# A gated recurrence on one core: VectorE takes x's sums with the bias from PSUM, update gates ahead of tanh, m by chunk and batch, a later wait for y, the last rows not moved

## What is computed

```python
def step(h, x_t):
    fused = sigmoid(concat([x_t, h]) @ w_W + w_b)
    hidden_state, output_state = split(fused, 2)
    memory_state = x_t @ wx_W + wx_b + hidden_state * (h @ wh_W + wh_b)
    h_new = output_state * h + (1.0 - output_state) * tanh(memory_state)
    return h_new, h_new
out = x + swapaxes(scan(step, cond_1024, swapaxes(x, 0, 1)), 0, 1)
```

## Time and profile before

| what | value |
|---|---|
| median of three runs | 1776.34 us |
| the profiled execution's own time | 1774.11 us |
| its span, first to last instruction | 1772.1 us |
| mean granted TensorE clock | 0.993 |
| busy share of the span: PE / PEld / DVE / ACT / POOL | 96 / 77 / 66 / 51 / 39 % |

### The profile page before, as it was taken

One profiled execution on the slowest core, in us unless ns is written; L12 is line 12 of the kernel. 1 busy time (PEld: TensorE's weight loads), 2 busy tenths in 40 slices (PEclk: granted clock), 3 DMA queues, 4 the chain that ended last, 5 costly groups with the idle time before them and its releaser, 6 DMA issues.

```text
span 1772.1 us, 211898 instructions
## 1 busy us (share of the span) xinstructions
PE 1697.1 (96%) x94336; PEld 1359.4 (77%) x94336; DVE 1174.3 (66%) x5144; ACT 910.5 (51%) x4749; POOL 694.7 (39%) x2699
## 2 busy tenths in 40 slices
PE   4999999999999999999999999999999999999997
PEld 2777777777777777777777777777777777777775
DVE  3666666666666666666666666666666666666665
ACT  2455555555555555555555555555555555555554
POOL 1334344333443433443343443334434434434433
PEclk8999999999999999999999999999999999999999
DMA  6111111111111111111111111111111111111111
GB/s 188 31 44 48 46 39 38 48 47 44 48 35 45 43 49 46 44 36 47 44 48 46 39 38 48 47 44 48 35 44 43 50 46 44 36 47 44 48 46 38
DMA packets 195513, 83.66 MB, mean 47 GB/s; under 512 B 123568, under 2 KB 194992, under 8 KB 195504
## 3 DMA queue, kind: packets, MB, share of 16 engines
q1 hardware_dynamic: 194448, 82.87, 17.3%
q10 hardware_dynamic: 1056, 0.67, 0.1%
HBM read 49.50 MB, written 33.95 MB: 47 GB/s over the span
## 4 chain that ended last, share of the span: by engine, by line
PE 59%; DVE 25%; issue 5%; POOL 4%; ACT 4%; DMA 1%; POOLq 1%; ACTq 0%; SPq 0%; DVEq 0%
PE ps L265 37%; PE ps L274 12%; PE ps L256 9%; DVE h L464 6%; DVE m_pre L450 5%; DVE turned_rm L439 5%; DVE turned_r L432 4%; DVE m_pre_parts L456 2%; DVE turned_m L435 2%; POOL y L552 2%; ACT m_by L362 2%; ACT h_by L369 2%; POOL h L542 2%; DVE turned_z L443 1%; POOL h L544 1%
## 5 line engine op out<-in xcount | busy, mean ns | idle before, releaser
L265 PE MATMUL ps<-wh,h 128*8 128x64 f32 x65536 | 1209.5, 220 | 56.9 <-DVE h L464 37.1
L265 PEld LDWEIGHTS ps<-wh,h 128*8 128x8 f32 x65536 | 960.3, 93 | 387.6 <-DVE h L464 327.0
L542 POOL TENSOR_TENSOR h<-h 128x16 f32<-128x16 f32 x1026 | 224.9, 219 | 985.1 <-DVE h L464 980.4
L274 PE MATMUL ps<-w_parts,h 128*24 128x128 bf16 x24576 | 531.8, 219 | 0.0
L274 PEld LDWEIGHTS ps<-w_parts,h 128*24 128x24 bf16 x24576 | 431.0, 121 | 0.0
L256 PE MATMUL ps<-wx,x_grp 128*32 128x384 f32 x4096 | 424.4, 486 | 0.0
L464 DVE TENSOR_TENSOR_SCAN h<-h_by,h 128x48 f32<-128x48 f32 x1024 | 258.8, 253 | 216.8 <-ACT h_by L369 216.8
L362 ACT ACTIVATE m_by<-turned_r 128x16 f32<-128x16 f32 x512 | 120.6, 236 | 504.7 <-DVE turned_r L432 504.7
L432 DVE STREAM_TRANSPOSE turned_r<-ps 128x64 f32<-128x64 f32 x512 | 127.9, 250 | 320.4 <-PE ps L265 212.6
L544 POOL TENSOR_TENSOR h<-h 128x16 f32<-128x16 f32 x1026 | 225.1, 219 | 80.4
L443 DVE STREAM_TRANSPOSE turned_z<-ps 128x64 f32<-128x64 f32 x1024 | 237.2, 232 | 2.6 <-PE ps L265 2.5
(11 more groups left out here) (32 smaller groups left out, 531.8 us busy)
## 6 DMA issues: line engine op xcount, KB each, us to landing
x_rows<-xs_biased SPq DMA_DIRECT2D x129, 192.0 KB, 1.9
ahead<-x_rows SPq DMA_DIRECT2D x516, 32.0 KB
ahead<-x_rows SPq DMA_DIRECT2D x1032, 8.0 KB
x_sb<-in_x SPq DMA_DIRECT2D x34, 256.0 KB, 3.1
x_grp<-in_x SPq DMA_DIRECT2D x516, 16.0 KB, 1.7
out_h<-y SPq DMA_DIRECT2D x32, 256.0 KB, 2.7
wx<-in_w_x SPq DMA_DIRECT2D x4, 768.0 KB, 9.7
wh<-in_w_h SPq DMA_DIRECT2D x4, 512.0 KB, 7.3
```

The source lines that it names most:

```text
L265: mm = pe.matmul(ps[Q * j:Q * j + B, bank, 0:W], h_of(s - 1, k), wh[:, k, j, at:at + W], start=False, stop=(k == KC - 1), skip_group_check ...
L274: mm = pe.matmul(ps[Q * j:Q * j + PARTS * B, RM_BANK, 0:2 * W], parts_of(s - 1, k), w_parts[:, k, part, j], start=False, stop=(k == KC - 1 ...
L542: pool.tensor_tensor(mid(1, s, o), mid(0, s, o), mid_top(0, s, o), ALU.subtract).then_inc(left_once[o], 1)
```

## The change

Five edits, in the program's own terms.

1. **x's sums with the bias**: VectorE reads the products from PSUM, adds the bias and writes `xs_biased` in one instruction, behind mix_h(1) of each group's fourth step, after waits for the product and for the rows of the slot that was filled last. ScalarE's take_x, GpSimd's add_bias, the tile xs and the semaphore x_taken are gone; TensorE waits for x_biased in place of x_taken.
2. **Update gates ahead of tanh** on ScalarE, in both halves; mix_h waits for tanh first and then for the gates.
3. **m by chunk and batch**: turned_m and turned_rm, and what is computed from them up to tanh's input, lie by chunk and then batch; before it was batch and then chunk. h stays as it was, so tanh writes in another order of addresses than it reads.
4. **A later wait for y**: VectorE waits at every second step, for y of three steps before; before it was every fourth step, for y of the step before.
5. **SyncE's queue**: the rows of a block's last group are moved at the start of the next block's turn, behind the store of y and the load of x; the transfer that stood ahead of the loop is now the loop's first. So the rows that the last group of all would move are not moved. In the setup the second sum with the bias waits until slot 0 is loaded; before it waited until the rows were written.

```diff
@@ SyncE
-            sp.wait_ge(x_biased, 2)
-            sp.wait_ge(ahead_loaded[0], LANDED)
-            put_ahead(sp, 1, 2 * 16)
             with sp.Fori(0, BLOCKS) as i:
                 cols = bass.ds(sp.snap((i + 2) % BLOCKS * TOK), TOK)
                 sp.wait_ge(x_loaded, sp.snap(i * 16 + 16))
                 sp.dma_start(x_sb[:, :, cols], x_flat[:, :, cols]).then_inc(x_loaded, 16)
+                sp.wait_ge(x_biased, sp.snap(i * PER_BLOCK + 2))
+                put_ahead(sp, 1, sp.snap((i * PER_BLOCK + 2) * 16))
                 for g in range(PER_BLOCK):
...
-                    sp.wait_ge(x_biased, sp.snap(i * PER_BLOCK + (g + 3)))
-                    put_ahead(sp, g % SLOTS, sp.snap((i * PER_BLOCK + (g + 3)) * 16))
+                    if g < PER_BLOCK - 1:
+                        sp.wait_ge(x_biased, sp.snap(i * PER_BLOCK + (g + 3)))
+                        put_ahead(sp, g % SLOTS, sp.snap((i * PER_BLOCK + (g + 3)) * 16))
                 sp.wait_ge(y_added, sp.snap(i * STEPS + 2 * STEPS))
@@ TensorE
-                        pe.wait_ge(x_taken, taken)
+                        pe.wait_ge(x_biased, taken)
@@ ScalarE
-            def take_x():
-                return act.activation(xs[:, :], ps[:, X_BANK, 0:COLS], ACT.Copy).then_inc(x_taken, 1)
...
-                act.activation(m_by[:, :, 1].rearrange("p (b c) -> p c b", c=HC), turned_r[:, :, 0:B], ACT.Sigmoid)\
+                act.activation(m_by[:, :, 1].rearrange("p (c b) -> p c b", b=B), turned_r[:, :, 0:B], ACT.Sigmoid)\
...
-                n_twice = h[:, (s - 1) % RING, o, 1:1 + REGION].rearrange("p (i w) -> p i w", w=TRI)[:, :, 0::2]
-                pre = (m_pre[:, :, 1], m_pre_parts[:, :, PARTS])[o]
-                act.activation(n_twice, pre.unsqueeze(2).to_broadcast([P, HB, 2]), ACT.Tanh)\
+                n_twice = h[:, (s - 1) % RING, o, 1:1 + REGION].rearrange("p (b c w) -> p c b w", c=HC, w=TRI)[:, :, :, 0::2]
+                pre = (m_pre[:, :, 1], m_pre_parts[:, :, PARTS])[o].rearrange("p (c b) -> p c b", b=B)
+                act.activation(n_twice, pre.unsqueeze(3).to_broadcast([P, HC, B, 2]), ACT.Tanh)\
...
                 reset_first()
+                act.wait_ge(z_turned[0], nxt)
+                update(0)
                 act.wait_ge(m_pre_ready[0], nxt)
                 new(0, s)
-                act.wait_ge(z_turned[0], nxt)
-                update(0)
...
                 put_rm(slot, t)
+                act.wait_ge(z_turned[1], nxt)
+                update(1)
                 act.wait_ge(m_pre_ready[1], nxt)
                 new(1, s)
-                act.wait_ge(z_turned[1], nxt)
-                update(1)
                 put_z(slot, t)
-                if s % RING == RING - 1:
-                    act.wait_ge(x_product, held(act, i * PER_BLOCK + (s // RING + 3)))
-                    act.wait_ge(x_biased, held(act, i * PER_BLOCK + (s // RING + 2)))
-                    take_x()
@@ VectorE
-                return dve.transpose(turned_m.rearrange("p g (b c) w -> p c g w b", c=HC),
+                return dve.transpose(turned_m.rearrange("p g (c b) w -> p c g w b", b=B),
...
-                return dve.transpose(turned_rm.rearrange("p g (b c) w -> p g c w b", c=HC),
-                                     ps[:, RM_BANK, 0:2 * W].rearrange("p (g c q) -> p g c q", g=2, q=Q))
+                return dve.transpose(turned_rm.rearrange("p g (c b) w -> p (g c) w b", b=B),
+                                     ps[:, RM_BANK, 0:2 * W].rearrange("p (c q) -> p c q", q=Q))
...
-                dve.wait_ge(z_ready[o], nxt)
                 dve.wait_ge(tanh_ready[o], nxt)
+                dve.wait_ge(z_ready[o], nxt)
...
+            def add_bias(bank):
+                dve.tensor_tensor(xs_biased[:, :], ps[:, bank, 0:COLS], bias_x[:, :], ALU.add).then_inc(x_biased, 1)
...
-                if s % RING == 0:
-                    dve.wait_ge(y_added, held(dve, t0 + (s + STEPS)))
+                if s % 2 == 0:
+                    dve.wait_ge(y_added, held(dve, t0 + (s + STEPS - RING + 2)))
...
                 mix_h(1, s, nxt)
+                if s % RING == RING - 1:
+                    g = s // RING
+                    dve.wait_ge(x_product, held(dve, i * PER_BLOCK + (g + 3)))
+                    dve.wait_ge(ahead_loaded[(g + 1) % SLOTS],
+                                held(dve, (i * (PER_BLOCK // SLOTS) + ((g + 1) // SLOTS + 1)) * LANDED))
+                    add_bias(X_BANK)
...
-            dve.wait_ge(x_left, 16)
-            add_bias(1)
+            dve.wait_ge(x_product, 2)
+            dve.wait_ge(ahead_loaded[0], LANDED)
+            add_bias(X_BANK + 1)
@@ GpSimd
-                    if s % RING == RING - 1:
-                        g = s // RING
-                        pool.wait_ge(x_taken, held(pool, i * PER_BLOCK + (g + 3)))
-                        pool.wait_ge(ahead_loaded[(g + 1) % SLOTS],
-                                     held(pool, (i * (PER_BLOCK // SLOTS) + ((g + 1) // SLOTS + 1)) * LANDED))
-                        add_bias()
```

More of the change, by code:

```diff
@@ L81, in build @@
         bias_x = sb("bias_x", [P, COLS])
-        xs = sb("xs", [P, COLS])
         xs_biased = sb("xs_biased", [P, COLS])
@@ L164, in build @@
         x_used = [sem(f"x_used{k}") for k in range(KC - 1)]
-        x_taken = sem("x_taken")
         x_biased = sem("x_biased")
@@ L247, in _ @@
             for slot in range(SLOTS):
-                sp.wait_ge(ahead_loaded[slot], (GROUPS // SLOTS + 1) * LANDED)
+                sp.wait_ge(ahead_loaded[slot], (GROUPS // SLOTS + 1 - slot) * LANDED)
             sp.wait_ge(y_stored, 16 * (BLOCKS + 2))
@@ L460, in mix_h @@
             def mix_h(o, s, nxt):
+                dve.wait_ge(tanh_ready[o], nxt)
                 dve.wait_ge(z_ready[o], nxt)
-                dve.wait_ge(tanh_ready[o], nxt)
                 dve.tensor_tensor_scan(h[:, s % RING, o, 0:REGION], h_by[:, o].rearrange("p i w -> p (i w)"),
@@ L466, in mix_h, with step @@
                     .then_inc(h_ready[o], 1)
-            def step(t0, s):
+            def add_bias(bank):
+                dve.tensor_tensor(xs_biased[:, :], ps[:, bank, 0:COLS], bias_x[:, :], ALU.add).then_inc(x_biased, 1)
+            def step(i, t0, s):
                 nxt = held(dve, t0 + (s + 1))
                 dve.wait_ge(r_done, nxt)
-                if s % RING == 0:
-                    dve.wait_ge(y_added, held(dve, t0 + (s + STEPS)))
+                if s % 2 == 0:
+                    dve.wait_ge(y_added, held(dve, t0 + (s + STEPS - RING + 2)))
                 turn_r().then_inc(r_turned, 1)
@@ L515, in _ @@
             dve.wait_ge(bias_x_loaded, 16)
-            add_bias(0)
+            dve.wait_ge(x_product, 1)
+            add_bias(X_BANK)
             for k in range(KC):
@@ L531, in _ @@
                 for s in range(STEPS):
-                    step(t0, s)
+                    step(i, t0, s)
         @block.gpsimd
         def _(pool):
-            def add_bias():
-                pool.tensor_tensor(xs_biased[:, :], xs[:, :], bias_x[:, :], ALU.add).then_inc(x_biased, 1)
             def part(o, s, after):
```

## The result

The changed kernel takes 1674.84 us, median of four runs (1674.5 to 1676.02), against 1776.03 us of the kernel before on the same chip. The ratio is 0.9431, with a 95% interval of 0.9414 to 0.9447: about 101 us less. The forecast was 1649 us, 1622 to 1692. Sign and range held; the gain was 101 us where 127 were forecast. The time lies above the forecast's own 1635 to 1660, and its nearest neighbour among the rivals is "rows late" with 1668.

What follows compares the result with a forecast made beforehand. TensorE was taken as near its limit in a ring of 3.25 us a step, with only 0.17 idle ahead of r(1). From 1774.1: -59.7 - 66.6 - 7.3 + 6 = 1646.5, with 2.2 for the median 1649 us; range 1622 to 1692.

Steps and rivals of the forecast that it cites:

- the forecast's own 1635 to 1660: Whole kernel: the main case's range around the predicted 1649 us, chance 0.5.
- rows late: Rival at block ends: rows 0.8 us late in place of 0.2 at 31 blocks, 1668 us; chance 0.15.
- the lock: Rival: VectorE's sum holds GpSimd's first half-1 subtraction, TensorE's parts 0.3 us late, 38 us, 1687 us; chance 0.1.
- The end of a group: Last step of each group: wait for y and GpSimd's sum go, 0.47 us each, 127 times, 59.7 us saved.
- y's 0.22: Group's end: m_pre comes 0.22 us late because the transpose of r waited for y.
- the lock's 0.25: Group's end: m_pre takes 0.47 us against 0.22 while GpSimd's bias sum runs, 0.25 more.
- Edit 2: ScalarE, half 1: gates fit in idle time ahead of tanh, mix_h(1) 0.13 us earlier, 512 times, 66.6 us saved.
- Tanh stays at 1003.91 to 1004.14: ScalarE, half 1: tanh keeps its start and end, so mix_h(1) begins at 1004.17 in place of 1004.30.
- Edit 3: m's layout: transpose gain taken as nothing, 31 us at most; tanh's 24-byte steps up to 10 us, taken as nothing.
- The argument on m's transpose: m's and z's transposes are each released by 16 matmuls, 0.21 us apart, so a shorter one moves nothing.
- Edit 5: SyncE's queue at block ends: rows land 0.2 us late, 31 times, 6 us cost; between 0 and 40 us.
- The end's 7.3 us: Kernel's end: without 13 row transfers ahead of it the last store is issued at once, 7.3 us saved.

Runs made afterwards that it cites:

- the kernel with two SBUF operands: Changed kernel with VectorE's loop sum reading both operands from SBUF, x's sums of all but the first two groups left out: 1703.99 us, ratio 0.9608.
- the old layout: Changed kernel with rows ahead of the store again and m's layout by batch and chunk in both halves: 1648.64 us, ratio 0.9290.
- Undone at rows that are in time: Changed kernel with rows ahead of the store again and tanh ahead of the update gates in both halves: 1709.59 us, ratio 0.9637.

## Why the prediction was right or wrong

The range held, but only in part for its reasons. The time is above the forecast's own 1635 to 1660 (chance 0.5) and above the 1668 of "rows late" (0.15); it is within 1622 to 1692 because that range reached up to the lock, which did not come. That was luck. The mechanism of "rows late" did come, with a mean wait of 0.73 us where it said 0.8.

**The end of a group** was right in its sum: 0.47 us gone, the new sum hidden, m_pre absorbing the rest. The split of the 0.47 was wrong: I priced y's 0.22 and the lock's 0.25 as two terms that add up. Alone the wait for y costs 0.20 and GpSimd's sum 0.47, and both together 0.47. The earlier trace rows had it already: m_pre ends at 1009.20 + 0.47 = 1009.67, 0.07 behind GpSimd's sum at 1009.60, so it is the sum's end that sets it.

**The lock** was rightly given no price. In the kernel with two SBUF operands GpSimd's subtraction grew, in the changed one it did not. The rule of the Trainium skill (SBUF — State Buffer, Who interferes with whom), that two SBUF inputs contend with GpSimd's reads and one does not, is borne out on both sides here: 0.47 against 0.22. The forecast price of the rival, 0.3 us a group, compares with 0.24 measured.

**Edit 2** was right in its mechanism and sized too high: 66.6 us forecast. Undone at rows that are in time it is 54. The step of the prediction that failed is "Tanh stays at 1003.91 to 1004.14": it takes 0.25 now, by edit 3, which makes mix_h(0) to mix_h(1) 1.01 in place of 0.98. With the old layout's 7 us added, edit 2 comes to 61; the rest of some 5 us, or 0.01 a step, stays open, at the edge of what the timeline's two decimals give. A plain step of 3.12 us was forecast; it is 3.14, and 3.13 with the old layout.

**Edit 3** I priced at nothing, with up to 10 us for tanh's 24-byte steps: about 7 us measured. The transpose of r and m gave no gain, as taken. The argument on m's transpose, which went from 298 to 234 ns, held: it moved nothing. Its shortening agrees with the Trainium skill (SBUF — State Buffer, the note on SBUF "cachelines"), by which an access that goes to a new line of 16 bytes pays. But as the recorded length of the transpose of r and m changed with its neighbours, such a record is no clean price of a layout.

**Edit 5** was the term that missed most: 6 us forecast, 18 measured, still within its own 0 to 40. Count from T, the start of mix_h(1) at a block's end, as the prediction does. In the block shown the write went out at T + 3.51 (3.3 forecast: the store was issued 0.32 behind y, for which nothing was allowed). It took 3.23 to land (1.9 and 0.6 forecast, where up to 1.3 was given for the load ahead). The reads' issues span 3.78 (3.76 before), and the last read landed some 1.6 later (1.9 forecast). So the rows were in at about T + 12.15 (11.45 forecast) and put_first began there; without the wait of 0.88 it would have begun at T + 11.3 (11.2 forecast). The error was to take the middle of an unknown at a deadline that was met within tenths: there each tenth that is wrong costs 31 tenths. The end's 7.3 us came as 7.0.

Together: 12 us from the rows and about 12 from edits 2 and 3 make up all but 2 of the 26 us between forecast and measurement.

## What to carry to other kernels

A transfer moved behind others in one queue is paid in issue time, in the bytes ahead of it and in the speed-up of the rest: work out its deadline with the new step, not the old, and put small urgent transfers ahead of large ones that nobody waits for. Where two waits end at the same instruction, don't add their prices: the one that ends last sets the time. Cutting only the one that ends first gains nothing (edit 4 without edit 1), and cutting only the other gains down to the first (edit 1 without edit 4: 0.27 of the 0.47 us). And an edit that is worth 54 us alone can show 45 in a kernel in which something else is late.

## What the runs showed of the hardware

A scan with two SBUF operands beside a 1.01 us GpSimd instruction was recorded with 0.70 us and ended 0.07 behind it; the other way round GpSimd's 0.22 became 0.47 behind VectorE's 0.55. From the issue of the 192 KB write to the first read back it took 1.9 us with no large transfer just ahead of it, 2.4 behind a 256 KB store issued 1.14 before, and 3.1 on the mean (2.7 to 3.4) behind a store and a 256 KB load. Tanh of 32 elements a partition, each written twice, took 248 ns where neighbours lay 24 bytes apart and 234 where 12. The transpose of m took 298 ns in steps of 16 bytes in the kernel before and 234 in steps of 8 in the change. A met semaphore wait behind one just ended put a VectorE transpose off by 0.09 us. Why the same transpose is recorded with 423 or 403 ns by what stands ahead of it was only argued, from its unchanged end.
